# Linear attention with decay and a mixture of experts: chunks of 64 tokens in 64x64 tiles, one more pipeline step

## What is computed

```python
q, k = elu(h @ Wq) + 1, elu(h @ Wk) + 1        # (8, 16 heads, 2048, 64)
v = h @ Wv
a = sigmoid(h @ Wa + ba + 2.0)                 # one decay for each head and token
def step(carry, inp):                          # over the tokens
    S = at * S + kt[:, None] * vt[None, :]     # 64 x 64
    z = at * z + kt
    return (S, z), (qt @ S) / (qt @ z + 1e-6)
x = x + ga * (out @ Wo)
```

## Time and profile before

| | |
|---|---|
| median of 3 runs | 3955.44 us (3953.79 to 3961.55) |
| the profiled execution | 3952.49 us, its span 3950.6 us |
| mean granted TensorE clock | 0.984 |
| busy, whole span: PE / PEld / DVE / ACT / POOL | 3504.8 / 2916.9 / 2878.1 / 1621.8 / 896.7 us |
| phase one, last residual | from 0 to 3045 us |
| phase two | from 3045 to 3951 us |

### The profile page before, as it was taken

How to read it: one execution, slowest core, us unless ns; L and a number is a source line. 1 busy time by engine, 2 the same in 40 slices (tenths; PEclk the granted TensorE clock), 3 DMA queues, 4 the chain that set the end, 5 groups by cost and what they waited for, 6 DMA issues and landing times. The chain is left out here.

```text
span 3950.6 us, 117499 instructions
## 1 busy us (share of the span) xinstructions
PE 3504.8 (89%) x46506; PEld 2916.9 (74%) x46506; DVE 2878.1 (73%) x6705; ACT 1621.8 (41%) x4044; POOL 896.7 (23%) x731
## 2 busy tenths in 40 slices
PE   7988898988888888888898989898896899999998
PEld 5777777777777777777777777777776677777777
DVE  5777676767766676767676767676675888888887
ACT  4554454544444454544444445454542211111111
POOL 3222222222222222222222222222221112222222
PEclk9999999999999999999999999999998999999999
DMA  4222222222222222222222222222222111110110
GB/s 140 91 90 91 84 89 84 89 84 86 87 83 82 83 93 90 92 87 88 85 87 86 83 83 91 82 90 84 90 85 88 37 44 38 38 43 32 43 43 22
DMA packets 146132, 304.81 MB, mean 77 GB/s; under 512 B 17048, under 2 KB 69320, under 8 KB 145352
## 3 DMA queue, kind: packets, MB, share of 16 engines
q1 hardware_dynamic: 145608, 297.42, 22.8%
HBM read 261.69 MB, written 35.67 MB: 75 GB/s over the span
## 5 line engine op out<-in xcount | busy, mean ns | idle before, releaser
L372 POOL TENSOR_TENSOR qs_sb<-lam_bc,qk_sb 128x512 f32<-128x512 f32 x256 | 327.9, 1281 | 1836.9 <-DVE qk_sb L813 1836.9
L427 ACT ACTIVATE qk_sb<-bank 128x512 f32<-128x512 f32 x512 | 307.0, 600 | 979.4 <-PE bank L502 979.2
L808 DVE TENSOR_TENSOR_SCAN decay<-a_bc,eye 128x512 f32<-128x512 f32 x512 | 595.5, 1205 | 59.3 <-issue 55.4
L828 DVE TENSOR_TENSOR p_sb<-bank,decay 128x512 f32<-128x512 f32 x512 | 330.0, 686 | 308.8 <-PE bank L655 307.8
L1147 DVE SCALAR_TENSOR_TENSOR acc<-bank,comb,acc 128x256 f32<-128x256 f32 x1024 | 461.2, 477 | 93.7 <-PE bank L1061 86.6
L454 ACT ACTIVATE kd_sb<-bank,decay 128x64 f32<-128x64 f32 x2048 | 448.2, 331 | 159.1 <-PE bank L626 158.9
L1059 PE MATMUL bank<-ew_hi,h_hi 128*128 128x512 f32 x1024 | 420.4, 411 | 2.1 <-DVE ew_lo L1131 2.1
L1060 PE MATMUL bank<-ew_lo,h_hi 128*128 128x512 f32 x1024 | 408.3, 399 | 0.0
L1061 PE MATMUL bank<-ew_hi,h_lo 128*128 128x512 f32 x1024 | 407.7, 398 | 0.0
L606 PE MATMUL bank<-ident,o_sb 128*128 128x128 f32 x1024 | 166.5, 285 | 239.1 <-DVE qk_sb L811 236.9
L606 PEld LDWEIGHTS bank<-ident,o_sb 128*128 128x128 f32 x1024 | 108.9, 140 | 330.0 <-DVE qk_sb L811 327.3
(11 more groups left out here) (177 smaller groups left out, 7628.5 us busy)
## 6 DMA issues: line engine op xcount, KB each, us to landing
a_bc<-rows_dram SPq DMA_DIRECT2D x256, 512.0 KB, 3.4
lam_bc<-rows_dram SPq DMA_DIRECT2D x512, 128.0 KB, 3.8
x_in<-in_L_attn_x_dram SPq DMA_DIRECT2D x32, 512.0 KB, 4.7
x_res<-in_L_attn_x_dram SPq DMA_DIRECT2D x32, 512.0 KB, 3.8
x_dram<-x_res SPq DMA_DIRECT2D x32, 512.0 KB, 4.6
x<-x_dram SPq DMA_DIRECT2D x32, 512.0 KB, 3.3
out_dram<-x SPq DMA_DIRECT2D x32, 512.0 KB, 2.9
ew_raw<-in_L_ffn_expert_W_dram SPq DMA_DIRECT2D x8, 256.0 KB, 5.7
```

The lines of the kernel that those rows point to most:

```text
L372: pool.tensor_tensor(qs_sb[:, na, :], lam_bc[na][:, :], q_sb, ALU.mult).then_inc(qs_ready, 1)
L808: dve.tensor_tensor_scan(decay[:, hd, :], a_bc[na][:, hd, :], eye4[:, :, :].rearrange("p c i -> p (c i)"), 0.0, ALU.mult, ALU.add).then_in ...
L828: dve.tensor_tensor(p_sb[:, na, hd, :], S[hd][:, :], decay[:, hd, :], ALU.mult)\
```

## The change

Only phase one changes, apart from the names of the PSUM banks in phase two.

- Chunks have 64 tokens (CK), eight a group (NCK). Every product of the recurrence is a matmul of a 64x64 tile with 64 or 65 columns, 16 a family. `place` says where a chunk's keys lie: odd heads have their halves exchanged, chunk ch of head hd sits in row half (ch - hd) % 2. Their value columns are made from tokens shifted by 64 (h_hi and h_lo get 64 more columns, the first chunk again), their decays are stored in that order.
- The key transposes are plain matmuls with the identity, and they share a pair of banks with the scores: KTR in the first half of each bank, S in the second. DENSE is the second of these banks, so a dense job waits for kd_sb and p_sb. The two are issued together at the end of the step, and p_sb waits for kd_sb.
- One decay scan of 512 columns serves both heads, with an identity of 64 (eye8); p_sb is one instruction; the chain has eight links.
- Four pairs are in work: a is u+3, b (U and chain) u+2, c (NUM) u+1.
- Wo's first half is in step 7 of its own group, its second in step 0 of the next; both h jobs are in one place, into DENSE and a bank of U; z comes ahead of the first value job, a ahead of the second. Wo goes over the pairs outside and the two token blocks inside.
- ScalarE copies the transposed output twice (oT32, oT_hi); GpSimd makes the low part oT_lo at the start of its step, and qs_sb comes last there, behind residual, norm and low part of h.
- The rows of decays are stored in step 4, with seven DMAs; a_bc has half its size, in two DMAs. lam_row is one scan of 512.

```diff
-DENSE_JOBS = {(0, 0): ("wo", -1, 0), ...
+DENSE_JOBS = {(0, 0): ("wo", -1, 1), (0, 1): ("v", 0, 5), (1, 0): ("v", 0, 6), (1, 1): ("v", 0, 7), (2, 0): ("h", 1, 0),
+              (3, 0): ("z", 1, 0), (3, 1): ("v", 1, 0), (4, 0): ("a", 1, 0), (4, 1): ("v", 1, 1), (5, 0): ("v", 1, 2),
+              (6, 0): ("v", 1, 3), (7, 0): ("v", 1, 4), (7, 1): ("wo", 0, 0)}
...
-        Q, K, SA, SB, KTR, NUM, DENSE = bank
+        Q, K, SCORES, UPAIR, NUM = bank
+        DENSE = SCORES[:, 1, :]
+        KTR, S = SCORES[:, :, 0:GT // 2], SCORES[:, :, GT // 2:GT]
+        HT = [DENSE, UPAIR[:, 0, :]]
+        U = [UPAIR[:, ch % 2, ch // 2 * VW:(ch // 2 + 1) * VW] for ch in range(NCK)]
...
+        def place(hd, ch):
+            m = (ch - hd) % NCK
+            return m % 2, m // 2
...
 # TensorE, one step
                     project(Ta, sa, pa, "wk", K, k_ps)
                     after(pe, q_ready, a)
                     project(Ta, sa, pa, "wq", Q, q_ps)
+                if dense_at(T, s, u, 0)[0]:
+                    after(pe, kd_ready, free)
+                    after(pe, p_ready, free)
                 dense_job(T, s, u, 0)
...
+                if exists(Tc):
+                    pe.wait_ge(qs_ready, c + 1)
+                    pe.wait_ge(state_step, c * NCK + NCK - 1)
...
+                        for hd in range(2):
+                            mm = pe.matmul(NUM[rows[ch % 2], hd, ch // 2 * VW:(ch // 2 + 1) * VW], qs_sb[rows[hd], pc % 2, query],
+                                           state[rows[hd], :], start=(ch < 2), stop=False)
...
+                            mm = pe.matmul(U[ch][rows[hd], :], kd_sb[rows[half], t, rows[hd]], v_sb[rows[half], t, v_col(pb, hd), :],
+                                           start=True, stop=True)
...
+                            mm = pe.matmul(NUM[rows[ch % 2], hd, ch // 2 * VW:(ch // 2 + 1) * VW], p_sb[rows[half], pc % 2, hd, t, :],
+                                           v_sb[rows[half], t, v_col(pc, hd), :], start=False, stop=(ch >= NCK - 2))
...
+                            pe.matmul(KTR[rows[half], hd, t * CK:(t + 1) * CK], k_sb[rows[hd], ch * CK:(ch + 1) * CK], ident[rows[hd], rows[hd]],
+                                      start=True, stop=True)
...
+                            mm = pe.matmul(S[rows[half], hd, t * CK:(t + 1) * CK], k_sb[rows[hd], tok], q_sb[rows[hd], tok], start=True, stop=True)
...
 # TensorE, value job 0 waits for z_out in the same step, job 1 for a_row and lam_row
+                if half == 0 and t == 0:
+                    pe.wait_ge(zb_ready, T + 1)
+                elif half == 0 and t == 1:
+                    pe.wait_ge(a_row_ready, T + 1)
+                    pe.wait_ge(lam_row_ready, T + 1)
...
 # VectorE, one step: k_sb, q_sb, one scan, dense outputs, chain(Tb), den to o_sb of Tc, then p_sb
+                    dve.wait_ge(decay_ready, a + 1)
+                    dve.wait_ge(kd_ready, a + 1)
+                    dve.tensor_tensor(p_sb[:, na, :, :, :].rearrange("p h t i -> p h (t i)"), S,
+                                      decay[:, :, :, :].rearrange("p h t i -> p h (t i)"), ALU.mult).then_inc(p_ready, 1)
...
 # GpSimd, one step: oT_lo, residual (u=0), norm (u=1), low part of h (u=2), qs_sb
+                    pool.wait_ge(oT32_ready, n + 1)
+                    pool.wait_ge(oT_hi_ready, n + 1)
+                    pool.tensor_tensor(oT_lo[:, u, :], oT32[:, :], oT_hi[:, u, :].bitcast(F32), ALU.subtract).then_inc(oT_lo_ready, 1)
...
 # ScalarE, one step: K and Q (Q waits for the last qs_sb), value copy or h, oT32 and oT_hi, z, kd_sb
+                    after(act, oT_lo_ready, n)
+                    act.wait_ge(oT_ps, n + 1)
+                    act.activation(oT32[:, :], K[:, :], ACT.Copy).then_inc(oT32_ready, 1)
+                    act.activation(oT_hi[:, u, :], K[:, :], ACT.Copy).then_inc(oT_hi_ready, 1)
```

More of the change, by code:

```diff
@@ L41 @@
 CH = 128
-HALF = CH // 2
+CK = 64
 SLICE = CH // 4
@@ L466, in step @@
                     act.activation(a_tok[:, :, :], a_tok[:, :, :], ACT.Exp, scale=-1.0).then_inc(z_exp, 1)
+                if exists(Ta):
+                    if isinstance(Ta, int) and a == 0:
+                        act.wait_ge(gates_stored, 16)
+                    act.wait_ge(decay_ready, a + 1)
+                    act.wait_ge(s_ps, a + 1)
+                    for t in range(NCH):
+                        for hd in range(2):
+                            ins = act.activation(kd_sb[:, t, hd * DH:(hd + 1) * DH],
+                                                 KTR[:, hd, t * CK:(t + 1) * CK], ACT.Copy,
+                                                 scale=decay[:, hd, t, CK - 1:CK])
+                    ins.then_inc(kd_ready, 1)
             attention_steps(act, step)
@@ new lines, in step @@
+                if exists(Tb):
+                    pe.wait_ge(kd_ready, b + 1)
+                    if isinstance(Tb, int) and b == 0:
+                        pe.wait_ge(ones_ready, 1)
+                    pe.wait_ge(v_ready, Tb * 8 + (NCH if pb < PAIRS // 2 else 2 * NCH))
+                    after(pe, state_step, b * NCK)
+                    if u == 2 and exists(T + 1):
+                        pe.wait_ge(h32_ready, (T + 2) * 2)
+                    pe.sem_inc(inputs_seen)
+                    for ch in range(NCK):
+                        for hd in range(2):
+                            half, t = place(hd, ch)
+                            mm = pe.matmul(U[ch][rows[hd], :], kd_sb[rows[half], t, rows[hd]], v_sb[rows[half], t, v_col(pb, hd), :],
+                                           start=True, stop=True)
+                    mm.then_inc(u_ps, 1)
@@ new lines, in step @@
+                if exists(Tc):
+                    pe.wait_ge(inter_ps, c + 1)
+                    pe.wait_ge(p_ready, c + 1)
+                    pe.sem_inc(inputs_seen)
+                    for ch in range(NCK):
+                        for hd in range(2):
+                            half, t = place(hd, ch)
+                            mm = pe.matmul(NUM[rows[ch % 2], hd, ch // 2 * VW:(ch // 2 + 1) * VW], p_sb[rows[half], pc % 2, hd, t, :],
+                                           v_sb[rows[half], t, v_col(pc, hd), :], start=False, stop=(ch >= NCK - 2))
+                    mm.then_inc(num_ps, 1)
@@ L645, in step @@
-                if exists(Ta):
-                    pe.wait_ge(q_ready, a + 1)
-                    after(pe, p_ready, 2 * a)
-                    pe.sem_inc(inputs_seen)
-                    for ch in range(NCH):
-                        tok = slice(ch * CH, (ch + 1) * CH)
-                        for half in range(2):
-                            keys = slice(ch * CH + half * HALF, ch * CH + (half + 1) * HALF)
-                            for hd in range(2):
-                                rows = head_rows[hd]
-                                mm = pe.matmul(S[hd][halves[half], tok], k_sb[rows, keys], q_sb[rows, tok], start=True, stop=True)
-                    mm.then_inc(s_ps, 1)
```

561 lines of the change are left out of this document (281 added, 280 removed).

## The result

The changed kernel took 4018.53 us (median of 4 runs, 4010.48 to 4028.18), the kernel before 3954.61 us beside it (4 runs, 3951.31 to 3961.55). The ratio is 1.016 with an interval of 1.0134 to 1.0187: slower by 1.6%, outside the range and on the side to which the prediction gave 0.13. The profiled execution took 4028.18 us, its span is 4026.3 us and its mean granted clock 0.943, where before had 0.984.

A forecast was written before the change was run, and what follows sets the result against it. It took VectorE's serial work, in a ring with TensorE, as the bound. Steps of 88.1 plus 0.6 for the clock saved 4.7 us a group, 146 over 31: 3952.5 - 146 + 8 = 3814, forecast 3815, range 3670 to 3940.

The forecast's parts named there:

- the prices of the parts: Per step: each small TensorE family 0.5 us, one decay scan 1.17, VectorE's chain of eight links 2.5.
- a plain step of 7.8: Steps u=5 and u=6, one value job each: 7.8 us against 9.8 before; k_sb every 7.5 to 8.2.
- the waits of u=3 and u=4: Value job at u=3 waits for z_out, TensorE still some 5 us; at u=4 it follows the lam scan.
- Rival 3: The 64x64 tiles run one after another: a family takes 2.1 us, not 0.5; 4210 us in all; chance 0.12.
- rival 2: U and inner numerator at half concurrency, row groups sharing a bank: 1.04 us, not 0.52; 3940 in all; chance 0.16.
- Hidden at the start: The added pipeline step costs between 0 (hidden in weight loads) and a full 10 us; 8 was taken.
- The walk: Eight steps of a group added up, each until p_sb's end: 88.1 us, with 13.7 at u=3 and 11.8 at u=4.
- 4.7 us a group saved: Steady groups: 88.7 us predicted against 93.4 measured before; 146 us over 31 groups.
- I take 0.6: Clock term per group: one more half-clock stretch costs at most 1.9 us; 0.6 was added to 88.1.
- VectorE's ring: In a plain step VectorE's serial work sets the 7.8 us; TensorE's work, to 7.6, is covered by 0.2.
- Rival 1: GpSimd's stalls do not bite: u=2 8.9, u=3 11.0, 84.2 us a group, 3675 to 3690 in all; chance 0.15.
- Rival 4: Handovers (semaphores, two engines on one bank) eat 0.6 us a step; little gain, 3950 in all; chance 0.05.

The follow-up runs named there:

- e7: The kernel before with its loop written out on every engine, nothing else changed: 3868.8 us, ratio 0.9782 to the kernel before.
- e12: The changed kernel with its loop written out and 12 and 5 discarded matmuls ahead of the value jobs of u=3 and u=4: 3847.34 us, ratio 0.9724.
- e5: The changed kernel with its loop written out on every engine: 3922.28 us, ratio 0.9925 to the kernel before.
- e8: e2 with the low part of o back on VectorE, without the copy oT32: 3823.28 us, ratio 0.9665 to the kernel before.
- e11: e2 with its loop written out (3729.9 us) and the key transposes issued twice: 3881.09 us, ratio 0.9812 to the kernel before.
- e2: The changed kernel with the old job order at u=3 and u=4 (value jobs ahead of z and a): 3824.93 us, ratio 0.9669 to the kernel before.
- e10: e2 with its loop written out (3729.9 us), both halves of Wo in step 0 and a value job in step 7: 3753.49 us, ratio 0.95.

## Why the prediction was wrong, point by point

**Right: the prices of the parts.** Small families of 0.5, one scan of 1.2, a chain of 2.5, a plain step of 7.8 (in the mean 8.1 at u=5, and 8.6 at u=6, outside the 7.5 to 8.2 that was to show it), the waits of u=3 and u=4, at u=3 with the releasers that the prediction named (at u=4 the profile names none). Rival 3 (tiles one after another) is out by the same rows. So is rival 2: U has four tiles, two of different row groups in each of its two banks, and its 32 records take 0.47 us, not 1.04; the key transposes, with one row group to a bank, take 0.48. The Trainium skill (TensorEngine Tiling, Restrictions and Gotchas) says that different row tiles can't access one PSUM bank at the same time; by that U would have taken twice as long, and in this trace it does not. "Hidden at the start" would have been better than 8 us: 1.3. (TensorE's step before, given as 8.3, adds up to 8.4 by its own prices; nothing rests on it.)

**Wrong, first: the comparison of the sum.** The walk gave 88.1 us for a group whose steps follow each other, and "giving 88.7 and 4.7 us a group saved" set it against 93.4, which contains half a jump of the loop. Like against like, the kernel before takes 90.9 us a group with its loop written out (e7, the same k_sb distances), so 88.7 meant 2.2 us saved and not 4.7: 68 us, and with the prediction's own 8 and 3 us for the edge and the median near 3895. The jump was in the trace of before (16.5 us of waits without releaser in 1000 us) and I had priced it nowhere. It accounts for 96.3 - 92.6 = 3.7 us of the 96.3 - 88.7 = 7.6 us a group by which the forecast missed.

**Wrong, second: the clock.** "I take 0.6" for one more stretch at half clock. The stall at u=3 brings one, that at u=4 another, and behind the first not some matmuls but the whole value job and three families run slow. Measured: 335 us of 2600 at 1.2 GHz in place of 58. Giving TensorE work in those stalls, with the waits left where they were, recovered 2.3 us a group (e12 against e5): 3.1 in the two steps, less 0.8 given back elsewhere. The term should have been 2.3 to 3; that 0.6 was taken is another 1.7 us of the miss.

The rest is 92.6 - 88.1 - 2.3 = 2.2 us a group, and e12, with the clock up and no loop, shows where. u=0, 2, 3 and 4 come out equal to the walk or up to 0.4 us under it; u=1, 5, 6 and 7 are 0.6 to 0.9 longer. In the plain steps (8.5 and 8.7 in e5 where the walk has 7.8) TensorE has no slack, and waits without releaser inside the small families add up to 0.8 and 1.1 us a step in e5's trace, as much as the walk lacks. What lengthens u=1 and u=7 stays open. On the page of the changed kernel the waits without releaser are 83.6 us ahead of L760 and 17.5 ahead of L734, over the whole run; before had 12.3 (L655) and 21.2 (L663). The changed kernel has 59,306 matmul records in place of 46,506. That these waits are the supply of instructions was not tried and stays open.

**Wrong, third: what sets the step.** The prediction followed VectorE's ring and gave TensorE as "covered by 0.2 only". With oT_lo back in the ring nothing changed (e8, where ScalarE and GpSimd had less to do as well), and 0.48 us more on TensorE cost 0.7 us in the plain steps (e11). TensorE's stream is the bound of the plain step, and the trace of the changed kernel agrees: 7.96 of 8.00 us busy, VectorE 6.82.

**Not wrong, but not seen: where the loss is made.** The walk has 13.7 + 11.8 = 25.5 us for u=3 and u=4 and says why. Had I walked the old order as well (measured, 21.9 in e2), the order could have stood out as a part of the change that loses. Measured, the change is +194 us for the order of z, a and the value jobs, and -130 us for everything else together (e2 against before); of that some 23 us is Wo over two steps (e10) and nothing the low part on GpSimd (e8). The 194 us hold the stalls, the half clock behind them and what the late q_sb adds to both. How the remaining 107 us divide between 64-token chunks and the additional pipeline step was not tried.

Rival 1, that GpSimd's stalls do not bite, is refuted: they do, and moving qs_sb mostly exchanges which operation is late. Rival 4, handovers that eat 0.6 a step, has the size of what the plain steps lost (8.1 to 8.7 for 7.8), but the trace shows it as waits without releaser inside the families and not as handovers between them.

## What to carry to other kernels

When steps are walked, set the walk against a walk of the kernel before and not against its measured time, and price the loop's edge and the clock after each stall as terms of their own. A job that waits for a result of the same step stalls the engine behind it: issue first what is ready, and last what another engine has still to answer. Before a part is called hidden, double it and see whether the time moves.

## What the runs showed of the hardware

- Kept as a loop of 14 passes, the steps cost this program 84, 95 and 96 us more than written out, 6 to 7 us a pass. In the changed kernel 3.4 us of it is a wait of TensorE without releaser, behind which it restarts at half clock.
- Discarded matmuls in two stalls a group made the kernel 75 us faster (e12 against e5), while the mean granted clock of the run rose from 0.953 to 0.984.
- Two row groups of 64x64 tiles writing different partitions of one PSUM bank kept the rate (32 records in 0.47 us, 0.48 with one row group to a bank).
- GpSimd's oT_lo took 1.81 us at 1359.65 in place of 1.30 while VectorE's scan with two SBUF inputs ran (from 1359.18, 1.21 us). Over the run, 33 of its 256 have more than 0.3 us of such a scan beside them and take 1.80 us in the mean, 173 have none and take 1.27. The Trainium skill (SBUF — State Buffer, Who interferes with whom) says that a VectorE instruction with two SBUF inputs contends with a GpSimd instruction that reads SBUF; the trace agrees.
